# Row chunk by row chunk: another order for the matmuls of the last three hidden blocks

## The chip, the cores and the metric

The kernel runs on one core of a Trainium2 chip. The metric is the device time of one execution in microseconds (us): the median over several runs, set beside the kernel before it on the same chip. One further execution was recorded by the hardware profiler; every duration in this text comes from that recording.

## What is computed

The reference is one layer with two residual steps. The second is the one that matters here:

```python
x = x + tanh(g_xattn) * attention(layernorm(x), ctx, ...)
x = x + tanh(g_ffn) * ffn(layernorm(x), gate_w, w1, w2)

def ffn(x, gate_w, w1, w2):                 # x: (2, 2048, 512), 8 experts
    probs = softmax(einsum('ntd,ed->nte', x, gate_w))
    g, m = top_k(probs.transpose(0, 2, 1), 512)       # each expert picks 512 rows per batch item
    xin = x[batch, m]
    h = gelu(einsum('nekd,edf->nekf', xin, w1))       # 512 -> 2048
    h = einsum('nekf,efd->nekd', h, w2)               # 2048 -> 512
    return zeros.at[batch, m].add(g[..., None] * h)
```

The cross-attention and the choice of the rows take the first part of the kernel and are not touched.

## The kernel before, in words

**Tiling.** The experts' work is cut into 16 groups, one for each expert `e` and batch item `b` (`g = 2e + b`). A group has 512 rows, in `NC = 4` chunks of 128, and 2048 hidden columns, in `KF = 16` blocks of 128. Every float32 product is made as three matmuls from a high and a low part of each operand (high x high, high x low, low x high). From expert 1 on, the first GEMM (`products_pe`) makes the hidden values of both batch items at once; those of item 1 stay in the tile `hid1` until its second GEMM.

**The second GEMM** is `output_pe` (line 1308). One call takes one step `s`, which is one hidden block: it waits until the block's low part of the hidden values is there (`h_split`, line 1311) and, from step 4 on, until the block of `w2` has been split (`w2_low`, line 1317). Then it goes over the four chunks of rows. Each chunk has a PSUM bank of its own (`Y_BANKS[c]`), and three matmuls of 128 x 512 add into it. So a step is 12 matmuls, and each bank gets three of them in every step. What is told of them:

```python
                if s == KF - 1 and c < NC - 1:
                    last.then_inc(y_chunk, 1)
            last.then_inc(y_sum, 1)
```

The semaphore `y_chunk` tells that a chunk is finished, which happens only in step 15; `y_sum` counts finished steps, and its last value tells that chunk 3 is finished.

**Buffers.** The tiles `hh` (high part of the hidden values) and `w2hl` (both parts of `w2`) have four slots, taken in turn by `s % 4` and `f % 4`. Slot reuse is guarded by `y_sum`: `high_second_act` (line 1294) may write `hh` for step `s` once step `s - 4` is finished, and `w2_high_act` (line 1161) likewise. On ScalarE the high part of `w2` (line 1165) and then the high part of the hidden values (line 1298) are made; VectorE follows with the two low parts (lines 1170 and 1303). SyncE loads the blocks of `w2` ahead of them (line 1085). In item 1 the blocks are taken from 15 down to 0, so the last step, 15, works on block 0.

**The end of a group.** `output_rows` (line 1335) multiplies a chunk by its rows' gates, out of the bank into `y`: chunks 0 and 1 on ScalarE (line 1345), chunks 2 and 3 on VectorE (line 1347). Then `scatter_pool` (line 1423) on GpSimd adds the chunk to the output rows in device memory with one indirect DMA with addition (line 1430), whose descriptors GpSimd makes. The four scatters of a group stand in order in GpSimd's queue. Each first waits for its own chunk and for all scatters of the group before. After the last group's four scatters the kernel ends: SyncE waits for all of them to have landed (lines 1811 and 1812).

**Order.** Nothing plans the work at run time: each engine's order is the order of the calls in `expert_pe`, `expert_act`, `expert_dve`, `expert_pool` and `expert_sp`. In the call for expert 7 (`final`) no later expert's work is mixed in.

Of the kernel before, what the change touches and what calls it, by code (L numbers as in the profile page):

```python
# [16 lines left out]
P = 128  # L17
# [11 lines left out]
def wait(eng, sem, value):  # L29

    if not isinstance(value, int) or value > 0:
        eng.wait_ge(sem, value)
# [14 lines left out]
def flamingo_layer(nc, x, ctx_in, mask, g_xattn, g_ffn, Wq, bq, Wk, bk, Wv, bv, Wo, bo, gate_w, w1, w2, out):  # L47
# [5 lines left out]
    KF = F // P  # L53
# [5 lines left out]
    NC = CAP // P  # L59
# [19 lines left out]
    with whole:  # L79
        def sem(name):  # L80
            return whole.enter_context(nc.semaphore(name))

        def keep(name, shape, dt):
            return whole.enter_context(nc.sbuf_tensor(name, shape, dt))
# [69 lines left out]
        hid1_low = keep("hid1_low", [P, KF, CAP], F32R)  # L154
# [64 lines left out]
        w2hl = keep("w2hl", [P, 4, 2, D], F32R)  # L219
        HIGH, LOW = range(2)  # L220
# [4 lines left out]
        hh = keep("hh", [P, 4, CAP], F32R)  # L225
# [76 lines left out]
        h_split = sem("h_split")  # L302
# [7 lines left out]
        y_sum = sem("y_sum")  # L310
        y_chunk = sem("y_chunk")
# [642 lines left out]
        def choice_pe(pe, b, piece):  # L954
            if piece < STEPS:
                if b == 0 and piece == 0:
                    pe.wait_ge(consts, CONSTS)
                pe.wait_ge(bit_count, b * STEPS + piece + 1)
                total = CHOICE_BANK[:, 0:CANDS * E]
                if b == 0:  # L960
                    for t in range(TB):
                        last = pe.matmul(total.rearrange("p (c e) -> p c e", c=CANDS), ones_m[:, :],
                                         atleast[:, :, t, :],
                                         start=(t == 0), stop=(t == TB - 1))
                else:
                    last = pe.matmul(total, ones_m[:, :], count[:, :, :].rearrange("p c e -> p (c e)"),
                                     start=True, stop=True)
                last.then_inc(bit_total, 1)
            elif piece == STEPS:
                pe.wait_ge(pick_in, 3 * b + 1)  # L970
                running_place(pe, above, NE)
                pe.wait_ge(pick_in, 3 * b + 2)
                running_place(pe, tied, 0)
                pe.wait_ge(pick_in, 3 * b + 3)
                pe.matmul(CHOICE_BANK[:, 2 * NE:2 * NE + E], ones_m[:, :], count[:, 0, :], start=True, stop=True)\
                  .then_inc(pick_sum, 1)
# [22 lines left out]
        Y_BANKS = (bank[0], bank[1], bank[2], bank[3])  # L999
# [24 lines left out]
        TOKENS_AT = {1: 0, 4: 1, 7: 2, 10: 3}  # L1024
        PROMOTE_AT = 12
        RUN_ON = 2

        def is_plain(e):
            return isinstance(e, int) and e == 0
# [4 lines left out]
        def pairs_before(e, p):  # L1034
            return e * NP - NP + p

        def step_no(e, b, s):
            return e * 2 * KF + b * KF + s

        def block_of(e, b, s):  # L1040
            return s if is_plain(e) or b == 0 else KF - 1 - s
# [3 lines left out]
        def w2_no(e, b, f):  # L1045
            if is_plain(e):
                return KF * b + f
            return e * 28 + 4 + (f if b == 0 else KF + KF - 1 - REUSED - f)
# [24 lines left out]
        def wait_w2_low(eng, done):  # L1073

            if isinstance(done, int) and done <= W2_EARLY:
                wait(eng, w2_low_early, done)
            else:
                eng.wait_ge(w2_low, done - W2_EARLY)
# [215 lines left out]
        def high_second_act(act, e, s):  # L1294
            f = block_of(e, 1, s)
            act.wait_ge(c22_act if f % 2 else c12_act, pairs_before(e, f // 2) + 1)
            act.wait_ge(y_sum, step_no(e, 1, s) - 3)
            act.activation(hh[:, s % 4, :], hid1[:, f, :], ACT.Copy).then_inc(h_high, 1)  # L1298

        def split_second_dve(dve, e, s):  # L1300
            f = block_of(e, 1, s)
            dve.wait_ge(h_high, step_no(e, 1, s) + 1)
            dve.tensor_tensor(hid1_low[:, f, :], hid1[:, f, :], hh[:, s % 4, :].bitcast(F32), ALU.subtract)\  # L1303
               .then_inc(h_split, 1)
# [3 lines left out]
        def output_pe(pe, e, b, s, inside=None):  # L1308
            n, g = step_no(e, b, s), e * 2 + b
            f = block_of(e, b, s)  # L1310
            pe.wait_ge(h_split, n + 1)
            if is_plain(e) or b == 0:
                wait_w2_low(pe, w2_no(e, b, f) + 1)
                low = hid0_low[:, s % 4, :]
            else:
                if s >= REUSED:
                    wait_w2_low(pe, w2_no(e, b, f) + 1)
                low = hid1_low[:, f, :]
            for c in range(NC):
                if s == 0 and not (isinstance(g, int) and g == 0):  # L1320

                    pe.wait_ge(y_act if c < 2 else y_dve, g * 2 - 2 + c % 2 + 1)
                for hpart, part in ((HIGH, HIGH), (HIGH, LOW), (LOW, HIGH)):
                    high = hh[:, s % 4, c * P:(c + 1) * P]
                    last = pe.matmul(Y_BANKS[c][:, :], high if hpart == HIGH else low[:, c * P:(c + 1) * P],  # L1325
                                     w2hl[:, f % 4, part, :],
                                     start=(s == 0 and hpart == HIGH and part == HIGH),
                                     stop=(s == KF - 1 and hpart == LOW))
                if c == 0 and inside is not None:
                    choice_pe(pe, 1, inside)  # L1330
                if s == KF - 1 and c < NC - 1:
                    last.then_inc(y_chunk, 1)
            last.then_inc(y_sum, 1)

        def output_rows(eng, e, b, c, done):
            g = e * 2 + b
            if c < NC - 1:
                eng.wait_ge(y_chunk, g * (NC - 1) + c + 1)
            else:
                eng.wait_ge(y_sum, step_no(e, b, KF))  # L1340
            wait(eng, scattered[c], g * 16)
            eng.wait_ge(promoted[b], e + 1)
            gate = slot_gate[:, b, c:c + 1]
            if eng is nc.scalar:
                ins = eng.activation(y[:, c, :], Y_BANKS[c][:, :], ACT.Copy, scale=gate)  # L1345
            else:
                ins = eng.tensor_scalar(y[:, c, :], Y_BANKS[c][:, :], gate, None, ALU.mult)
            ins.then_inc(done, 1)
# [3 lines left out]
        def slots_pe(pe, g):  # L1352
            pe.wait_ge(hot, g + 1)
            for t in range(TB):
                last = pe.matmul(SLOT_BANK[:, 0:NC * NV], onehot[:, t, :],  # L1355
                                 carried[:, t, :, :].rearrange("p c v -> p (c v)"),
                                 start=(t == 0), stop=(t == TB - 1))
            last.then_inc(slots_sum, 1)
# [292 lines left out]
        def after_plain(e):  # L1651
            return isinstance(e, int) and e == 1
# [15 lines left out]
        def expert_pe(pe, e, final):  # L1668
            if not after_plain(e):
                products_pe(pe, e, 0)  # L1670
            for p in range(NP):
                if p + 1 < NP:
                    products_pe(pe, e, p + 1)
                if p in SLOTS_AT and not final:
                    pe.wait_ge(combined, (pairs_before(e, p) + 1) * COMBINED + U3_IS)
                    slots_pe(pe, e * 2 + 2 + SLOTS_AT[p])
                for s in (2 * p, 2 * p + 1):
                    output_pe(pe, e, 0, s)
            for s in range(KF):
                if s in TOKENS_AT and not final:  # L1680
                    operands_pe(pe, e + 1, TOKENS_AT[s])
                output_pe(pe, e, 1, s)

        def expert_act(act, e, final):
            if not after_plain(e):
# [4 lines left out]
            for p in range(NP):  # L1690
# [7 lines left out]
                if p + 1 < NP:  # L1698
                    for f in (2 * p + 2, 2 * p + 3):
                        w2_high_act(act, e, 0, f)  # L1700
                    hidden_act(act, e, p + 1)
            for s in range(RUN_ON):
                high_second_act(act, e, s)
            for c in (0, 1):
                output_rows(act, e, 0, c, y_act)
            for s in range(KF):
                if s in TOKENS_AT and not final:
                    operands_high_act(act, e + 1, TOKENS_AT[s])
                if s + RUN_ON < KF:
                    high_second_act(act, e, s + RUN_ON)  # L1710
                if 1 <= s <= KF - REUSED:
# [6 lines left out]
        def expert_dve(dve, e, final):  # L1718
# [4 lines left out]
            for p in range(NP):  # L1723
# [9 lines left out]
                if p in SLOTS_AT and not final:  # L1733
                    slots_dve(dve, e + 1, SLOTS_AT[p])
            for s in range(RUN_ON):
                split_second_dve(dve, e, s)
            for c in (2, 3):
                output_rows(dve, e, 0, c, y_dve)
            for s in range(KF):
                if s in TOKENS_AT and not final:  # L1740
                    operands_mix_dve(dve, e + 1, TOKENS_AT[s])
                if s + RUN_ON < KF:
                    split_second_dve(dve, e, s + RUN_ON)
                if 1 <= s <= KF - REUSED:
# [204 lines left out]
```

## Time and profile before

| | us |
|---|---|
| median of 3 runs | 1564.37 |
| lowest, highest | 1562.61, 1566.11 |
| the profiled execution: time | 1563.59 |
| the profiled execution: span | 1561.8 |
| TensorE busy in the span | 1493.4 |
| mean granted TensorE clock | 0.987 |

The span runs from the first to the last recorded event; 1.8 us of the profiled execution's time lie outside it. The profiled execution is 0.8 us below the median. A granted clock of 1.0 is TensorE's full 2.4 GHz, 0.5 is 1.2 GHz. Matmuls overlap at their ends, so the time between the starts of two of them is shorter than the duration that a row shows. The DMA share is the mean over the 16 DMA engines. It can read a little over 1 in a short window.

### The profile page before, as it was taken

What the parts mean: (1) busy time and instruction counts of PE and PEld (TensorE: products, weight loads), DVE (VectorE), ACT (ScalarE), POOL (GpSimd) and SP (SyncE); (2) the same over time, 40 slices, a digit from 0 to 9 for tenths busy, and PEclk for the clock granted to TensorE, in tenths of its full rate; (3) what the DMA queues carried; (4) which work ended last, traced back from release to release, by engine and by line L of the source; (5) the groups of instructions that cost most, each with busy time, mean ns of one, the idle gap of its engine ahead of it and who ended that gap; (6) DMA issues with size and microseconds to landing.
All of it is one profiled execution on the core that took longest, in us unless ns stands there. A gap on an engine that the chain in (4) does not pass through costs nothing.

```text
span 1561.8 us, 22316 instructions
## 1 busy us (share of the span) xinstructions
PE 1493.4 (96%) x7169; PEld 1211.2 (78%) x7169; DVE 1015.7 (65%) x1716; ACT 732.8 (47%) x1347; POOL 593.7 (38%) x554
## 2 busy tenths in 40 slices
PE   6886699999999999999999999999999999999996
PEld 5654477787788888888888888888888888888885
DVE  2578776657766676676657676767667675766542
ACT  1385233445444554454445444455445444554432
POOL 2265555543544044323443244403531444323211
PEclk9999699999999999999999999999999999999998
DMA  7176423543333333245234423334324433442133
GB/s 229 55 255 204 162 88 99 141 138 82 89 120 62 101 97 95 93 88 116 82 108 81 110 91 99 74 95 103 100 76 95 110 96 93 82 108 81 42 78 70
DMA packets 101401, 163.58 MB, mean 105 GB/s; under 512 B 7411, under 2 KB 45315, under 8 KB 101285
## 3 DMA queue, kind: packets, MB, share of 16 engines
q1 hardware_dynamic: 86885, 128.50, 26.4%
q0 software_dynamic: 14400, 33.56, 11.9%
q8 instruction: 69, 1.13, 0.3%
q14 instruction: 47, 0.39, 0.1%
HBM read 128.48 MB, written 33.55 MB: 104 GB/s over the span
## 4 chain that ended last, share of the span: by engine, by line
PE 86%; DVE 7%; issue 2%; ACT 2%; POOL 1%; DMA 1%; POOLq 0%; SPq 0%; DVEq 0%; ACTq 0%
PE bank L1325 42%; PE bank L1211 33%; PE bank L1185 4%; PE bank L1480 2%; PE bank L572 1%; PE bank L590 1%; PE bank L400 1%; DVE st L817 1%; DVE onehot L1366 1%; ACT xT L641 1%; DVE sc L793 0%; DMA ctx_raw<-in_ctx 0%; PE bank L1355 0%; DVE w2hl L1170 0%; DVE hid_low L1203 0%
## 5 line engine op out<-in xcount | busy, mean ns | idle before, releaser
L1325 PE MATMUL bank<-w2hl,hh 128*128 128x512 f32 x2048 | 635.7, 392 | 0.0
L1211 PE MATMUL bank<-xo,whl 128*128 128x512 f32 x2352 | 543.0, 390 | 3.7 <-DVE mix L1275 2.8
L1211 PEld LDWEIGHTS bank<-xo,whl 128*128 128x128 f32 x2352 | 440.7, 188 | 98.5 <-DVE mix L1275 3.7
L1325 PEld LDWEIGHTS bank<-w2hl,hh 128*128 128x128 f32 x2048 | 380.4, 188 | 76.0
L1325 PE MATMUL bank<-w2hl,hid_low 128*128 128x512 f32 x1024 | 398.7, 389 | 0.0
L1325 PEld LDWEIGHTS bank<-w2hl,hid_low 128*128 128x128 f32 x1024 | 192.2, 188 | 40.4
L1430 POOL DMA_INDIRECT layer_out<-y,slot_row x64 | 103.2, 1613 | 301.8 <-ACT y L1345 287.0
L1170 DVE TENSOR_TENSOR w2hl<-raw,w2hl 128x512 fp32r<-128x512 f32 x213 | 147.7, 715 | 50.6 <-ACT w2hl L1165 41.3
L1139 POOL TENSOR_TENSOR whl<-raw,whl 128x512 fp32r<-128x512 f32 x56 | 82.1, 1466 | 258.2 <-ACT whl L1105 258.2
L1165 ACT ACTIVATE w2hl<-raw 128x512 fp32r<-128x512 f32 x228 | 136.5, 624 | 60.1 <-DMA raw<-in_L_ffn_w 43.9
L1144 POOL TENSOR_TENSOR whl<-wsum,whl 128x512 fp32r<-128x512 f32 x56 | 75.1, 1341 | 183.4 <-ACT whl L1126 183.4
L1250 ACT ACTIVATE mix<-bank 128x512 f32<-128x512 f32 x56 | 33.4, 596 | 200.4 <-PE bank L1211 200.3
L1257 ACT ACTIVATE hid<-bank 128x512 f32<-128x512 f32 x56 | 33.5, 599 | 157.5 <-PE bank L1211 157.5
L1278 DVE TENSOR_TENSOR mix<-bank,mix 128x512 f32<-128x512 f32 x56 | 38.8, 692 | 96.4 <-PE bank L1211 96.2
L1185 PE MATMUL bank<-xp,whl 128*128 128x512 f32 x384 | 94.3, 396 | 1.6 <-DVE xp L1452 1.6
L1303 DVE TENSOR_TENSOR hid_low<-hid,hh 128x512 fp32r<-128x512 f32 x112 | 86.8, 779 | 12.8 <-ACT hh L1298 12.8
L1275 DVE TENSOR_TENSOR mix<-bank,mix 128x512 f32<-128x512 f32 x56 | 38.5, 688 | 80.4 <-PE bank L1211 80.4
L1185 PEld LDWEIGHTS bank<-xp,whl 128*128 128x128 f32 x384 | 73.2, 191 | 17.6 <-DVE xp L1452 2.3
L1283 DVE TENSOR_TENSOR hid<-bank,mix 128x512 f32<-128x512 f32 x56 | 38.7, 692 | 67.3 <-PE bank L1211 67.3
L1291 DVE TENSOR_TENSOR hid_low<-hid,hh 128x512 fp32r<-128x512 f32 x112 | 80.0, 714 | 1.0 <-ACT hh L1266 1.0
L1146 POOL TENSOR_TENSOR whl<-wsum,whl 128x512 fp32r<-128x512 f32 x56 | 76.4, 1364 | 0.0
L1126 ACT ACTIVATE whl<-wsum 128x1024 fp32r<-128x1024 f32 x56 | 59.0, 1054 | 36.7 <-DVE wsum L1122 36.7
(224 smaller groups left out, 1783.0 us busy)
## 6 DMA issues: line engine op xcount, KB each, us to landing
raw<-in_L_ffn_w SPq DMA_DIRECT2D x228, 256.0 KB, 2.7
raw<-in_L_ffn_w SPq DMA_DIRECT2D x72, 512.0 KB, 4.9
x_s<-in_x SPq DMA_DIRECT2D x8, 1024.0 KB, 6.9
layer_out<-x SPq DMA_DIRECT2D x8, 1024.0 KB, 9.0
xn_rows<-xn SPq DMA_DIRECT2D x8, 1024.0 KB, 4.9
raw_k<-in_L_xattn_Wk SPq DMA_DIRECT2D x1, 1024.0 KB, 5.4
raw_q<-in_L_xattn_Wq SPq DMA_DIRECT2D x1, 1024.0 KB, 11.3
raw_v<-in_L_xattn_Wv SPq DMA_DIRECT2D x1, 1024.0 KB, 13.4
```

Of the source, the lines that this page charges most:

```text
L1126: act.activation(whl[:, p % 2, HIGH, 2 * S1:14, :], wsum[:, :, :], ACT.Copy).then_inc(w1_sum_high, 1)
L1139: pool.tensor_tensor(low[:, 2 * A11:2 * A11 + 4, :], raw1[:, p % 2, :, 0:P], high[:, 2 * A11:2 * A11 + 4, :], ALU.subtract)
L1144: pool.tensor_tensor(low[:, 2 * S1:2 * S1 + 4, :], wsum[:, 0:4, :], high[:, 2 * S1:2 * S1 + 4, :], ALU.subtract)
L1146: pool.tensor_tensor(low[:, 2 * S3:2 * S3 + 4, :], wsum[:, 4:8, :], high[:, 2 * S3:2 * S3 + 4, :], ALU.subtract).then_inc(w1_low, 1)
L1165: act.activation(w2hl[:, f % 4, HIGH, :], raw2[:, slot, :], ACT.Copy).then_inc(w2_high, 1)
L1170: eng.tensor_tensor(w2hl[:, f % 4, LOW, :], raw2[:, slot, :], w2hl[:, f % 4, HIGH, :].bitcast(F32), ALU.subtract).then_inc(w2_low_early if ...
L1185: last = pe.matmul(H_BANKS[f % 2][:, :], whl[:, p % 2, part, 2 * k + f % 2, :], xp[:, b, xpart, k, :], start=(k == 0 and part == HIGH and ...
L1211: last = pe.matmul(bk[:, :], whl[:, p % 2, part, 2 * w + k, :], xo[:, xpart, x, k, :], start=(not adds and k == 0 and part == HIGH and xpa ...
L1291: dve.tensor_tensor(hid0_low[:, f % 4, :], hid0[:, f % 4, :], hh[:, f % 4, :].bitcast(F32), ALU.subtract)\
L1303: dve.tensor_tensor(hid1_low[:, f, :], hid1[:, f, :], hh[:, s % 4, :].bitcast(F32), ALU.subtract)\
L1325: last = pe.matmul(Y_BANKS[c][:, :], high if hpart == HIGH else low[:, c * P:(c + 1) * P], w2hl[:, f % 4, part, :], start=(s == 0 and hpar ...
L1430: pool.indirect_dma_start(out_rows, bass.IndirectOffsetOnAxis(ap=slot_row[:, b, c:c + 1], axis=0), y[:, c, :], None, compute_op=ALU.add).t ...
```

## The change

In the call for the last expert, item 1, steps 0 to 12 are as before. The 36 matmuls of steps 13, 14 and 15 are issued by a new function, `last_blocks_pe`, with the loops exchanged: chunk outside, step inside. It first waits for the hidden values and the `w2` blocks of all three steps, then adds nine matmuls into bank 0 and tells `y_chunk`, nine into bank 1, nine into bank 2, nine into bank 3. The last matmul of each step in chunk 3 raises `y_sum`. The number of matmuls, their operands and what each bank sums is the same, and within a bank so is the order. No other engine's program is changed.

```diff
+        ENDING = 3
...
+        def last_blocks_pe(pe, e):
+            ends = range(KF - ENDING, KF)
+            for s in ends:
+                pe.wait_ge(h_split, step_no(e, 1, s) + 1)
+                wait_w2_low(pe, w2_no(e, 1, block_of(e, 1, s)) + 1)
+            for c in range(NC):
+                cs = slice(c * P, (c + 1) * P)
+                for s in ends:
+                    f = block_of(e, 1, s)
+                    for hpart, part in ((HIGH, HIGH), (HIGH, LOW), (LOW, HIGH)):
+                        last = pe.matmul(Y_BANKS[c][:, :], hh[:, s % 4, cs] if hpart == HIGH else hid1_low[:, f, cs],
+                                         w2hl[:, f % 4, part, :], start=False, stop=(s == KF - 1 and hpart == LOW))
+                    if c == NC - 1:
+                        last.then_inc(y_sum, 1)
+                if c < NC - 1:
+                    last.then_inc(y_chunk, 1)
...
-            for s in range(KF):
+            for s in range(KF - ENDING if final else KF):
                 if s in TOKENS_AT and not final:
                     operands_pe(pe, e + 1, TOKENS_AT[s])
                 output_pe(pe, e, 1, s)
+            if final:
+                last_blocks_pe(pe, e)
```

TensorE before, from the start of step 13 of the last group (`bank0` to `bank3` are the banks of chunks 0 to 3, `hh` the high and `hid1_low` the low part of the hidden values):

```order
L1325 MATMUL bank0<-w2hl,hh 128x512 [waits w2_low,h_split]
L1325 MATMUL bank0<-w2hl,hh 128x512
L1325 MATMUL bank0<-w2hl,hid1_low 128x512
L1325 MATMUL bank1<-w2hl,hh 128x512 x2
L1325 MATMUL bank1<-w2hl,hid1_low 128x512
L1325 MATMUL bank2<-w2hl,hh 128x512 x2
L1325 MATMUL bank2<-w2hl,hid1_low 128x512
L1325 MATMUL bank3<-w2hl,hh 128x512 x2
L1325 MATMUL bank3<-w2hl,hid1_low 128x512
L1325 MATMUL bank0<-w2hl,hh 128x512 [waits w2_low,h_split]
```

The step gives three matmuls to each bank, and the next step begins with bank 0 and its own waits.

TensorE with the change, from the same place:

```order
L1348 MATMUL bank0<-w2hl,hh 128x512 [waits w2_low,h_split]
L1348 MATMUL bank0<-w2hl,hh 128x512
L1348 MATMUL bank0<-w2hl,hid1_low 128x512
L1348 MATMUL bank0<-w2hl,hh 128x512 x2
L1348 MATMUL bank0<-w2hl,hid1_low 128x512
L1348 MATMUL bank0<-w2hl,hh 128x512 x2
L1348 MATMUL bank0<-w2hl,hid1_low 128x512
L1348 MATMUL bank1<-w2hl,hh 128x512 x2
```

Bank 0 now gets nine matmuls before bank 1 gets its first, and the waits for all three steps stand ahead of the first.

TensorE with the change, at its very end:

```order
L1348 MATMUL bank2<-w2hl,hid1_low 128x512
L1348 MATMUL bank3<-w2hl,hh 128x512 x2
L1348 MATMUL bank3<-w2hl,hid1_low 128x512
L1348 MATMUL bank3<-w2hl,hh 128x512 x2
L1348 MATMUL bank3<-w2hl,hid1_low 128x512
L1348 MATMUL bank3<-w2hl,hh 128x512 x2
L1348 MATMUL bank3<-w2hl,hid1_low 128x512
```

Bank 3 gets all of its last nine matmuls at the end of the program, where before each bank had three of the last twelve.

## Rows read from the trace of the kernel before

**Rows 1.** The page: busy us and share of the span, then the chain's shares.
```profile
PE 1493.4 (96%) x7169; PEld 1211.2 (78%) x7169; DVE 1015.7 (65%) x1716; ACT 732.8 (47%) x1347; POOL 593.7 (38%) x554
...
PE 86%; DVE 7%; issue 2%; ACT 2%; POOL 1%; DMA 1%; POOLq 0%; SPq 0%; DVEq 0%; ACTq 0%
```

**Rows 2.** The chain that ended last, from 1540 us (start us, us, what).
```profile
1539.95 7.72 PE bank L1325 x34
...
1551.06 1.55 POOL layer_out L1430
...
1554.78 1.56 POOL layer_out L1430
```

**Rows 3.** Timeline, all engines, 1539 to 1562 us (start us, us, engine, line, operation).
```profile
1538.85 0.63 ACT L1165 ACTIVATE w2hl<-raw 128x512 fp32r<-128x512 f32 x1 [1.56 <-PE bank L1325]
...
1540.13 0.68 DVE L1303 TENSOR_TENSOR hid_low<-hid,hh 128x512 fp32r<-128x512 f32 x1
...
1541.15 0.41 PEld L1325 LDWEIGHTS bank<-w2hl,hh 128*128 128x128 f32 x2
1541.37 0.62 PE L1325 MATMUL bank<-w2hl,hh 128*128 128x512 f32 x2
...
1543.18 0.39 PE L1325 MATMUL bank<-w2hl,hid_low 128*128 128x512 f32 x1
...
1545.22 0.39 PE L1325 MATMUL bank<-w2hl,hid_low 128*128 128x512 f32 x1
...
1547.27 0.39 PE L1325 MATMUL bank<-w2hl,hid_low 128*128 128x512 f32 x1
...
1547.69 1.37 ACT L1345 ACTIVATE y<-bank,slot_gate 128x512 f32<-128x512 f32 x2 [7.69 <-PE bank L1325]
...
1549.05 1.43 DVE L1347 TENSOR_SCALAR y<-bank,slot_gate 128x512 f32<-128x512 f32 x2 [8.24 <-PE bank L1325]
...
1549.20 1.55 POOL L1430 DMA_INDIRECT layer_out<-y,slot_row  x1 [35.62 <-ACT y L1345]
1549.31 0.39 PE L1325 MATMUL bank<-w2hl,hid_low 128*128 128x512 f32 x1
```

**Rows 4.** Lines 1345 and 1347 in the last 22 us (ns min/median/max, first and last start).
```profile
L1345 ACT ACTIVATE y<-bank,slot_gate x2: 689/689/689, 1547.7 to 1548.4; 128x512 f32<-128x512 f32 x2
L1347 DVE TENSOR_SCALAR y<-bank,slot_gate x2: 751/751/751, 1549.1 to 1549.7; 128x512 f32<-128x512 f32 x2
```

**Rows 5.** Windows 1549.2 to 1559.9 us: length, five engines' busy us, PEclk, DMA share, GB/s.
```profile
1549.20:1551.30 2.10, 0.49 (x3) 0.07 (x1) 1.28 (x2) 0.00 (x0) 1.79 (x2) 1.00 0.00 0
1551.30:1559.90 8.60, 0.00 (x0) 0.00 (x0) 0.00 (x0) 0.00 (x0) 4.43 (x3) 0.56 0.98 123
```

**Rows 6.** Line 1430, the last group's first two scatters: issue to landing.
```profile
DMA to landing us min/median/max: 5.2/5.4/5.5
```

**Rows 7.** Line 1430, its last two scatters: issue to landing.
```profile
DMA to landing us min/median/max: 5.7/5.7/5.7
```

**Rows 8.** Chain of GpSimd, 313 to 316 us: twelve matmuls into one bank.
```profile
313.01 2.72 PE bank L1185 x12
```

**Rows 9.** Line 1085, the last load of a w2 block (ns, start; us to landing).
```profile
L1085 SPq DMA_DIRECT2D raw<-in_L_ffn_w x1: 328/328/328, 1534.8 to 1534.8; - x1
...
DMA to landing us min/median/max: 2.6/2.6/2.6
```

**Rows 10.** Line 1085, all 228 loads of a w2 block: us to landing.
```profile
DMA to landing us min/median/max: 2.5/2.7/6.9
```

**Rows 11.** Windows after the last matmul, columns as in rows 5.
```profile
1551.00:1552.00 1.00, 0.00 (x0) 0.00 (x0) 0.00 (x0) 0.00 (x0) 0.94 (x1) 1.00 0.98 72
...
1552.50:1553.00 0.50, 0.00 (x0) 0.00 (x0) 0.00 (x0) 0.00 (x0) 0.19 (x2) 0.50 1.08 197
```

**Rows 12.** Timeline of TensorE, 183 to 187 us, at a granted clock of 0.50.
```profile
183.17 4.13 PE L1185 MATMUL bank<-xp,whl 128*128 128x512 f32 x9 [1.56 <-DVE xp L1452]
```

## The prediction

> **What bounds the kernel now.** The page comes first. TensorE is busy for 96% of the span and is 86% of the chain that ended last [rows 1], so anywhere in the middle only TensorE's own time counts, and the change leaves its 36 matmuls what they were. The end of the chain tells something else [rows 2]: TensorE's last piece in it ends at 1547.67 us, and after that only GpSimd appears, with scatters at 1551.06 and 1554.78 us. TensorE itself works on until 1549.31 + 0.39 = 1549.70 us [rows 3]. So the last chunk's matmuls are not what the end waits for: the end waits for four scatters in a row, and these wait for chunk 0.
>
> The timeline of the last 23 us shows why [rows 3]. All four chunks are finished within the last step: chunk 0 at 1547.27 + 0.39 = 1547.66 us, chunk 3 at 1549.70 us, 2.04 us apart. Eviction on ScalarE starts 0.03 us after chunk 0's last matmul, takes 0.69 us [rows 3, 4], and the first scatter starts at 1549.20 us, 0.82 us after it. The scatters follow each other by (1554.78 - 1549.20) / 3 = 1.86 us [rows 2, 3]. GpSimd has every later chunk ready before it can take it; it is a queue that began too late.
>
> Below the scatters lie the DMA engines. They move nothing until 1551.30 us, 2.10 us after the first scatter's start, and are then 98% busy for 8.60 us [rows 5]. Four scatters in 8.60 us are 2.15 us each, more than the 1.86 us between two issues, so work piles up in front of them. The first two scatters land 5.5 and 5.2 us after their starts, the last two 5.7 us [rows 6, 7]. The last lands at 1554.78 + 5.7 = 1560.48 us, and 1.3 us later the span of 1561.8 us ends.
>
> **The change, step by step.** Matmuls start (1549.31 - 1541.37) / 35 = 0.227 us apart [rows 3]. Exchanging the loops leaves the 36 starting points and gives them to other chunks: chunk 0 has the first nine, and so on. Every ninth one is a row of the timeline, which gives the new finishing times: chunk 0 at 1543.18 + 0.39 = 1543.57, chunk 1 at 1545.22 + 0.39 = 1545.61, chunk 2 at 1547.66, chunk 3 at 1549.70 us as before. Chunk 0 gains 4.09 us, chunk 3 nothing.
>
> *The new waits.* Steps 14 and 15 must be ready before step 13 starts. The last thing that they need is the low part of step 15's hidden values, finished at 1540.13 + 0.68 = 1540.81 us; the first weight load of step 13 is at 1541.15 us [rows 3]. That is 0.34 us to spare, so I cost the waits at nothing, with 0 to 0.3 us as bounds (six semaphore waits in a row, at the 0.03 us that a hand-over took above, are 0.2). Behind these waits stand only TensorE's last 36 matmuls. ScalarE and VectorE have nothing between 1540.81 us and the evictions, so nobody is held up by the later end of steps 13 and 14.
>
> *Nine matmuls into one bank.* Twelve in a row into one bank took 2.72 us [rows 8], which is 12 x 0.227: the same pace as over four banks. Cost nothing; bounds 0 and, at a rounding of 0.01 in 2.72 us, 0.03 us. The Trainium skill says otherwise (Perfetto Trace Analysis, Matmul Optimizations): all eight PSUM banks should be in use to have as much parallelism as possible. By that rule grouping nine on one bank would slow TensorE, by a price the page doesn't give. This trace does not agree at these sizes.
>
> *The scatters.* Each starts at the later of two times: its own chunk's finish + 0.03 + eviction (0.69 on ScalarE, 0.75 on VectorE [rows 4]) + 0.82, or 1.86 us after the scatter before it.
> Scatter 0: 1543.57 + 1.54 = 1545.11.
> Scatter 1: 1545.61 + 1.54 = 1547.15 (queue 1546.97).
> Scatter 2: 1547.66 + 1.60 = 1549.26 (queue 1549.01).
> Scatter 3: 1549.70 + 1.60 = 1551.30 (queue 1551.12).
> The last scatter starts 1554.78 - 1551.30 = 3.48 us earlier. From there TensorE is the bound again: chunk 3's last matmul, its eviction, its scatter.
>
> *The landing of the last scatter.* Here the trace leaves a choice. If it again takes 5.7 us, the gain is 3.48 us. If the DMA engines set the end, their 8.60 us begin at 1545.11 + 2.10 = 1547.21 and end at 1555.81 instead of 1559.90 us: 4.09 us. Scatters now come 2.06 us apart, nearly the engines' own 2.15, so the last one meets a backlog of 1547.21 + 3 x 2.15 - (1551.30 + 2.10) = 0.26 us, where it had 1551.30 + 3 x 2.15 - (1554.78 + 2.10) = 0.87 us. I take the middle, 3.8 us, because the first scatter, with no backlog at all, still took 5.5 us, only 0.2 less than the last.
>
> Sum: 0 (waits) + 0 (bank) - 3.8 us. The span becomes 1558.0 us, the profiled execution 1563.59 - 3.8 = 1559.8 us, and from the median, 0.8 us above that execution, 1564.37 - 3.8 = **1560.6 us**. What a measurement of this kernel can tell from no change is about 0.2%, 3.1 us; the three runs of before lie 3.5 us apart. The gain stands just above it.
>
> **The rivals.**
> *A: no backlog counts, 3.5 us.* For it: two scatters with little in front of them took 5.5 and 5.2 us and the two behind them 5.7, so what a scatter takes hardly depends on the backlog. Against: 98% busy engines for 8.60 us. Time: 1564.37 - 3.48 = 1560.9 us. The Trainium skill (DMA: Bandwidth & Descriptors, Anatomy of one DMA) has it this way: a fixed 2.0 us and the bytes at 436 GB/s, an estimate of 2.6 us for a scatter of 262,144 bytes, with 0.6 us of moving, so engines idle between issues. This trace shows 123 GB/s and 5.2 us at least.
>
> *B: the gathered wait is late, or hand-overs are slower than 0.82 us.* With 0.34 us to spare every delay of step 15's operands now goes straight to the end. The last `w2` load starts at 1534.8 and lands in 2.6 us, at 1537.4; ScalarE takes it at 1538.85 us [rows 3, 9]. Loads took up to 6.9 us [rows 10]. One that long would land at 1541.7, shift the operands by 2.85 us and hold TensorE for 2.5 us: gain 1.3 us, 1563.1 us. Against: the long ones lie beside scatters, and none is under way there. Two slow hand-overs of 0.8 us each would leave 2.2 us, 1562.2 us.
>
> *C: nothing is gained.* If GpSimd's start were held by something other than chunk 0 (the four waits for the scatters before, the gates' order), the four scatters would stay where they are: 1564.4 us. For it: the 0.82 us between eviction and scatter are unexplained. Against: they follow the eviction at once, after 35.62 us of waiting for ScalarE [rows 3].
>
> *D: slower, by the clock.* After its last matmul at 1549.70 us TensorE's granted clock was still 1.00 up to 1552.0 and 0.50 (1.2 GHz) from 1552.5 us [rows 11], so an idle time of 2.3 to 2.8 us halves it. At 0.50 nine matmuls took 4.13 us [rows 12], 0.459 each, 0.232 more than now. If B's hold of 2.5 us reaches that point, the 36 matmuls cost up to 36 x 0.232 = 8.4 us more: -3.8 + 2.5 + 8.4 = +7.1, 1571.5 us. It decides from a hold of 2.3 us on, if more than 19 of the 36 then run at half clock (2.5 + 19 x 0.232 - 3.8 = 3.1). Before the change the same late load would have had 5.4 us more room.
>
> **How the numbers follow.** Forecast 0.45, A 0.25, B 0.15, C 0.08, D 0.03; the 0.04 left is for a gain beyond 4.5 us. The forecast and A differ by 0.3 us and stand 0.4 to 0.7 us above the bound of 3.1; with medians that wander by about 1 us, some 0.85 of their 0.70 is measured as faster, 0.60, and with the 0.04 that is 0.64. B, C and the rest of the forecast and A are within 0.2%: 0.33. D is 0.03. The range takes the forecast with the ends 3.48 and 4.09, 1 us of measurement on both sides and most of B: 1559.0 to 1563.0 us. Left out are C, D and a bit of each tail.
>
> **What would show it.** In the profile after: the span ends 8.3 us after TensorE's last matmul, not 12.1; scatters start 2.0 to 2.1 us apart instead of 1.86, each 0.8 us behind an eviction; the chain's end runs through chunk 3's matmuls, VectorE's eviction and one scatter. The last landing takes 5.1 to 5.7 us, which tells the forecast from A. A gap on TensorE ahead of step 13 shows B; a granted clock below 1.00 before the last matmul shows D; scatters still 1.86 us apart and ending at the same time show C. I am wrong if the last scatter doesn't start 3.2 us or more earlier against TensorE's last matmul.

## The result, and the profile after

| | before | with the change |
|---|---|---|
| median, us | 1563.05 (10 runs) | 1559.09 (10 runs) |
| profiled execution: time, us | 1563.59 | 1557.74 |
| profiled execution: span, us | 1561.8 | 1555.9 |
| its last matmul ends, us | 1549.70 | 1547.77 |
| from there to the span's end (the tail), us | 12.10 | 8.13 |

The ratio is 0.9973, with a 95% interval of 0.9963 to 0.9983: 4.2 us less, between 2.7 and 5.8 us. The seven further runs of the kernel before brought its median from 1564.37 to 1563.05 us. One of them took 1906.81 us; it is not in the ratio, and the other nine runs, 1561.80 to 1566.11 us, have a median of 1562.74 us. Spans are read to 0.1 us, so a tail is good to about 0.05 us.

The page still names TensorE. Two lines of it, to be laid beside [rows 1] (busy us and share of the span; shares of the chain):

```profile
PE 1491.1 (96%) x7169; PEld 1209.0 (78%) x7169; DVE 1015.3 (65%) x1716; ACT 733.1 (47%) x1347; POOL 593.3 (38%) x554
...
PE 86%; DVE 7%; ACT 2%; issue 2%; POOL 1%; DMA 1%; POOLq 0%; SPq 0%; DVEq 0%; ACTq 0%
```

The middle hardly moved (0.6 us, worked out below). The timeline of the end, all engines (start us, us, engine, line, operation), answers to [rows 3]. The functions behind the new code have moved by 20 lines: 1345, 1347 and 1430 of before are 1365, 1367 and 1450 here.

```profile
1539.22 0.39 PE L1326 MATMUL bank<-w2hl,hid_low 128*128 128x512 f32 x1
...
1539.45 0.62 PE L1348 MATMUL bank<-w2hl,hh 128*128 128x512 f32 x2
...
1541.26 0.39 PE L1348 MATMUL bank<-w2hl,hid_low 128*128 128x512 f32 x1
...
1541.69 0.69 ACT L1365 ACTIVATE y<-bank,slot_gate 128x512 f32<-128x512 f32 x1 [3.61 <-PE bank L1348]
...
1543.20 1.55 POOL L1450 DMA_INDIRECT layer_out<-y,slot_row  x1 [31.54 <-ACT y L1365]
1543.30 0.39 PE L1348 MATMUL bank<-w2hl,hid_low 128*128 128x512 f32 x1
...
1545.24 1.55 POOL L1450 DMA_INDIRECT layer_out<-y,slot_row  x1 [0.49 <-issue]
1545.34 0.39 PE L1348 MATMUL bank<-w2hl,hid_low 128*128 128x512 f32 x1
...
1545.77 0.75 DVE L1367 TENSOR_SCALAR y<-bank,slot_gate 128x512 f32<-128x512 f32 x1 [6.88 <-PE bank L1348]
...
1547.34 1.56 POOL L1450 DMA_INDIRECT layer_out<-y,slot_row  x1 [0.55 <-DMA layer_out<-y,slot_row]
1547.38 0.39 PE L1348 MATMUL bank<-w2hl,hid_low 128*128 128x512 f32 x1
1547.81 0.75 DVE L1367 TENSOR_SCALAR y<-bank,slot_gate 128x512 f32<-128x512 f32 x1 [1.29 <-PE bank L1348]
1549.38 1.56 POOL L1450 DMA_INDIRECT layer_out<-y,slot_row  x1 [0.48 <-issue]
```

Step 13's first matmul starts at 1539.45 us, 0.23 us after step 12's last: no gap. The ninth matmul of each chunk ends at 1541.26 + 0.39 = 1541.65, then 1543.69, 1545.73 and 1547.77 us, 2.04 us apart. Each eviction starts 0.04 us after its chunk, and the first scatter 0.82 us after its eviction. Scatters follow each other by 2.04, 2.10 and 2.04 us. The last one starts 1.61 us after the last matmul; before it was 5.08 us after it. So it moved by 3.47 us, where 3.48 was worked out.

The windows of the DMA engines' work (length; busy us of TensorE, its weight loads, VectorE, ScalarE and GpSimd; granted clock; DMA share; GB/s) answer to [rows 5]:

```profile
1543.20:1545.30 2.10, 2.10 (x11) 1.75 (x10) 0.00 (x0) 0.69 (x1) 1.61 (x2) 1.00 0.00 0
1545.30:1553.90 8.60, 2.47 (x11) 1.69 (x10) 1.50 (x2) 0.00 (x0) 4.61 (x3) 0.76 0.96 122
```

The engines again begin 2.10 us after the first scatter's start and are busy for 8.60 us, 96% instead of 98%. Against the last matmul this stretch ends at 6.13 us instead of 10.20: 4.07 us earlier.

The chain that ended last needs a caution here (start us, us, what), beside [rows 2]:

```profile
1539.61 2.06 PE bank L1348 x9
...
1541.69 0.70 ACT y L1365
...
1543.20 4.15 DMA layer_out<-y,slot_row
1547.35 1.29 POOL layer_out L1450
```

It goes from chunk 0's nine matmuls over the first scatter's DMA to a later scatter. The program has no wait of one scatter for another of the same group; the scatter at 1547.34 us stands 0.82 us behind its own eviction, 1545.77 + 0.75. A landing merely fell into the same moment. The releasers in a chain are inferred, and this one is wrong. So the prediction's sign that the chain would end over chunk 3's matmuls, VectorE's eviction and one scatter did not appear; the timeline above shows that order, with 0.04 and 0.82 us between the three.

The span of this execution is 5.9 us shorter, but only 12.10 - 8.13 = 3.97 us of it is the tail. The other 1.9 us do not come from the end: the part before the experts was 2.5 us shorter, where no line of the change runs, and the middle gave 0.6 us back. The first row of the tile `onehot` in each of four executions, whose "first start" (167.7, 165.2, ...) marks the beginning of the experts' part: the kernel before, the change, the change with two steps (below), and the change once more:

```profile
L1366 DVE TENSOR_TENSOR onehot<-iota_slot,slot_lo x16: 2282/2284/3379, 167.7 to 1273.8; 128x2048 bf16<-128x2048 bf16 x16
L1386 DVE TENSOR_TENSOR onehot<-iota_slot,slot_lo x16: 2282/2285/3376, 165.2 to 1271.9; 128x2048 bf16<-128x2048 bf16 x16
L1386 DVE TENSOR_TENSOR onehot<-iota_slot,slot_lo x16: 2282/2284/3376, 168.7 to 1275.4; 128x2048 bf16<-128x2048 bf16 x16
L1386 DVE TENSOR_TENSOR onehot<-iota_slot,slot_lo x16: 2282/2284/3378, 164.9 to 1271.9; 128x2048 bf16<-128x2048 bf16 x16
```

The last matmul of these four ends at 1549.70, 1547.77, 1551.27 and 1547.79 us. Less the first start, that is 1382.0, 1382.6, 1382.6 and 1382.9 us. One execution differs from another by up to 4 us in its first 170 us, and by at most 0.9 us from there to the last matmul. So from here on the tail is compared, which leaves this out, beside the times.

### The profile page after: what moved, and what is told of

Its sections match the earlier page's. It is cut to its first block, busy times and chain, and to the rows that moved or that the text cites. A ratio compares the mean times of both kernels' runs of the same rounds, so it can differ in the third digit from the quotient of the medians.

```text
span 1555.9 us, 22316 instructions
## 1 busy us (share of the span) xinstructions
PE 1491.1 (96%) x7169; PEld 1209.0 (78%) x7169; DVE 1015.3 (65%) x1716; ACT 733.1 (47%) x1347; POOL 593.3 (38%) x554
## 4 chain that ended last, share of the span: by engine, by line
PE 86%; DVE 7%; ACT 2%; issue 2%; POOL 1%; DMA 1%; POOLq 0%; SPq 0%; DVEq 0%; ACTq 0%
PE bank L1326 42%; PE bank L1212 33%; PE bank L1186 4%; PE bank L1500 2%; PE bank L572 1%; PE bank L590 1%; DVE onehot L1386 1%; DVE st L817 1%; PE bank L400 1%; ACT xT L641 1%; DVE hid_low L1204 0%; DVE sc L793 0%; PE bank L1375 0%; DMA ctx_raw<-in_ctx 0%; DVE w2hl L1171 0%
## 5 line engine op out<-in xcount | busy, mean ns | idle before, releaser
L1326 PE MATMUL bank<-w2hl,hh 128*128 128x512 f32 x2024 | 628.4, 392 | 0.0
L1326 PEld LDWEIGHTS bank<-w2hl,hh 128*128 128x128 f32 x2024 | 376.0, 188 | 75.1
L1326 PE MATMUL bank<-w2hl,hid_low 128*128 128x512 f32 x1012 | 394.0, 389 | 0.0
```

## The experiments

All tails in one place. "Start" is the last scatter's start after the last matmul's end, "spacing" the time from the scatter before it, "issue to end" the tail less the start.

| run | spacing | start | tail | issue to end |
|---|---|---|---|---|
| before | 1.87 | 5.08 | 12.10 | 7.02 |
| waits only | 1.87 | 5.09 | 12.05 | 6.96 |
| two steps | 1.86 | 3.04 | 9.93 | 6.89 |
| the change | 2.04 | 1.61 | 8.13 | 6.52 |
| the change again | 2.04 | 1.61 | 8.31 | 6.70 |
| chunk wait last, first scatter | 2.05 | 1.62 | 8.33 | 6.71 |
| chunk wait last, later three | 2.04 | 1.70 | 8.32 | 6.62 |
| chunk wait last, all four | 2.04 | 1.70 | 8.15 | 6.45 |
| staggered | 2.72 | 1.61 | 7.83 | 6.22 |
| four steps | 2.72 | 1.62 | 7.78 | 6.16 |
| the change, last scatter alone | none | 1.61 | 7.64 | 6.03 |
| before, last scatter alone | none | 1.61 | 7.60 | 5.99 |

**Two steps.**

```diff
-        ENDING = 3
+        ENDING = 2
```

> Only steps 14 and 15 are exchanged (24 matmuls), not 13. With tail = time from the last matmul's end to the end of the span (12.1 us before, 8.1 us with the change). Chunk 0 is then finished 12 matmuls earlier than before, 2.72 us, chunk 1 8 matmuls... in full: first scatter 2.05 us earlier (chunk 0 after 6 of 24 matmuls: 9 x 0.227), and as chunks now come 1.36 us apart, the queue of scatters at 1.86 us is the limit again. Theory (the end follows the first scatter, through the DMA engines' 8.6 us): tail 12.1 - 2.05 = 10.05 us. Rival A (the end follows the last scatter's start, fixed landing): last scatter also 2.05 us earlier, the same 10.05. Rival C (order alone does nothing, the 4 us come from elsewhere): tail 12.1 or 8.1. Time 2 us below the kernel before.

(Its "12 matmuls earlier" for chunk 0 is a slip; nine matmuls, 2.05 us, is the difference, and the tail is worked out from that.)

Measured: tail 9.93 us, median 1560.68 us (8 runs), ratio 0.9982 (0.9971 to 0.9993), 2.8 us less than before. The timeline of GpSimd shows the queue (start us, us, ...; the third scatter is left out):

```profile
1548.73 1.55 POOL L1450 DMA_INDIRECT layer_out<-y,slot_row  x1 [33.58 <-ACT y L1365]
1550.59 1.55 POOL L1450 DMA_INDIRECT layer_out<-y,slot_row  x1 [0.30 <-issue]
...
1554.31 1.56 POOL L1450 DMA_INDIRECT layer_out<-y,slot_row  x1 [0.30 <-issue]
```

Scatters are 1.86 us apart: chunks finish faster than GpSimd issues, and it is a queue with an earlier start again. So 12.10 - 9.93 = 2.2 of the 4 us come from exchanging two steps, the rest from the third. Rival C is gone: the tail follows the number of steps exchanged.

**Four steps.**

```diff
-        ENDING = 3
+        ENDING = 4
```

> Four steps are exchanged, 12 to 15. The wait ahead of step 12 then needs step 15's hidden values, which are ready 2.0 us after step 11's end. Rival D and B's mechanism: TensorE idles 2.2 to 2.4 us ahead of step 12 (0 with the change as it is). If the granted clock stays at 1.00, the 48 matmuls keep 0.227 us and the end comes 2.2 to 2.4 us later than with three steps, less 0.1 to 0.3 us for a backlog that is gone: about 2.0 us below the kernel before. If the idle time halves the clock, the 48 matmuls cost up to 48 x 0.232 = 11 us more and the kernel is slower than before. I expect the clock to stay: tail 7.8 to 8.1 us.

Measured: tail 7.78 us, median 1562.11 us (10 runs), ratio 0.9994 (0.9984 to 1.0003). The timeline of TensorE at step 11's end and step 12's start:

```profile
1539.93 0.39 PE L1326 MATMUL bank<-w2hl,hid_low 128*128 128x512 f32 x1
1542.56 0.70 PE L1348 MATMUL bank<-w2hl,hh 128*128 128x512 f32 x2 [2.24 <-DVE hid_low L1304]
```

The idle time is 2.24 us, and what ended it is the hidden values' low part, as expected. The two windows that hold it and the 48 matmuls behind it (columns as above):

```profile
1540.00:1542.60 2.60, 0.36 (x3) 0.07 (x1) 1.29 (x2) 1.15 (x2) 0.00 (x0) 1.00 0.01 3
1542.60:1553.70 11.10, 11.10 (x48) 8.86 (x48) 0.75 (x1) 1.38 (x2) 4.18 (x3) 1.00 0.37 45
```

The granted clock stays at 1.00 in both. The 48 matmuls take 11.1 us, 0.23 each, so the hold costs its own length and not a doubled matmul time. In the times four steps give back most of the gain: 0.9 us below the kernel before by the ratio (between 2.5 less and 0.5 more), an interval that holds the 2.0 us expected; by the profile it is 12.10 - 7.78 - 2.24 = 2.1 us. Three is the largest number of steps that this order can take without a hold.

The same execution shows a scatter with nothing in front of it, though three went before. The DMA engines had run dry by the time the last scatter's data moved, 2.1 us after its start at 1555.34 us (columns as above):

```profile
1557.12:1557.22 0.10, 0.00 (x0) 0.00 (x0) 0.00 (x0) 0.00 (x0) 0.00 (x0) 1.00 0.00 0
...
1557.42:1557.52 0.10, 0.00 (x0) 0.00 (x0) 0.00 (x0) 0.00 (x0) 0.00 (x0) 1.00 3.50 143
```

**Waits only.** The steps in the old order behind the gathered waits:

```diff
-            for c in range(NC):
-                cs = slice(c * P, (c + 1) * P)
-                for s in ends:
-                    f = block_of(e, 1, s)
+            for s in ends:
+                f = block_of(e, 1, s)
+                for c in range(NC):
+                    cs = slice(c * P, (c + 1) * P)
...
-                    if c == NC - 1:
-                        last.then_inc(y_sum, 1)
-                if c < NC - 1:
-                    last.then_inc(y_chunk, 1)
+                    if s == KF - 1 and c < NC - 1:
+                        last.then_inc(y_chunk, 1)
+                last.then_inc(y_sum, 1)
```

> The waits of steps 13 to 15 all stand ahead of step 13, but the steps are taken as before. If the gathered waits cost nothing (0.34 us to spare), step 13's first matmul starts 0.227 us after step 12's last, and the tail is that of before, 12.1 us. If they cost, there is a gap ahead of step 13 of up to 0.3 us. The tail can't be 8.1 us if the order of the matmuls is what gains.

Measured: tail 12.05 us. TensorE's timeline, step 12's last matmul and step 13's first:

```profile
1539.70 0.39 PE L1326 MATMUL bank<-w2hl,hid_low 128*128 128x512 f32 x1
1539.93 0.62 PE L1348 MATMUL bank<-w2hl,hh 128*128 128x512 f32 x2
```

They start 0.23 us apart. The waits cost nothing, and without the exchanged loops they gain nothing.

**One scatter alone**, with the change and with the kernel before. The edit is the same in both:

```diff
-                for c in range(NC):
-                    scatter_pool(pool, e, 1, c)
+                scatter_pool(pool, e, 1, NC - 1)
...
-                sp.wait_ge(scattered[c], 16 * G)
+                sp.wait_ge(scattered[c], 16 * G if c == NC - 1 else 16 * G - 16)
```

> With the change, but the last group's scatters of chunks 0, 1 and 2 are left out (their rows lack the last expert's part). Nothing lies in front of the last scatter in the DMA engines. Theory (a backlog of about 0.26 us in front of the last scatter): tail 8.1 - 0.3 = 7.8 us, and the engines busy for about 2.15 us from 2.1 us after its start. Rival A (a scatter takes what it takes): tail 8.1 us. If the engines need less than 2.15 us for one scatter alone, then the rate of 122 GB/s was not theirs but that of the issues.

> The kernel before, with the last group's scatters of chunks 0, 1 and 2 left out (their rows lack the last expert's part). Chunk 3's last matmul is the last of all, as with the change, so if the order of the matmuls acts only through the scatters in front, the tail is the same as with the change and one scatter: 7.6 us, against 12.1 us with four scatters. If the old order costs anything else at the end, the tail is longer than 7.8 us.

Measured: tails of 7.64 and 7.60 us. The scatter with the change, and the windows after its start:

```profile
1549.77 1.55 POOL L1450 DMA_INDIRECT layer_out<-y,slot_row  x1 [37.73 <-DVE y L1367]
```

```profile
1549.80:1551.80 2.00, 0.00 (x0) 0.00 (x0) 0.00 (x0) 0.00 (x0) 1.52 (x1) 0.80 0.02 4
1551.80:1554.10 2.30, 0.00 (x0) 0.00 (x0) 0.00 (x0) 0.00 (x0) 0.00 (x0) 0.50 0.93 114
```

A single scatter begins in the DMA engines 2.0 us after its start and keeps them 93% busy for 2.30 us at 114 GB/s. So the rate of 122 GB/s in the full rows is the engines' own, not that of the issues, and a scatter every 1.86 us is more than they take. The tail of 7.64 us is 0.2 us under the 7.8 us of the theory and 0.5 us under rival A's 8.1 us. That the old and the new order agree, where with four scatters they lie 4 us apart, says that the order of the matmuls acts on the tail through the scatters in front, to within the 0.2 us to which a tail repeats (below).

**GpSimd's waits in another order.** Three kernels, for all four scatters of the last group, for the later three, and for the first:

```diff
+            chunk_last = isinstance(e, int) and e + 1 == E and b == 1
+            if not chunk_last:
+                pool.wait_ge(y_act if c < 2 else y_dve, g * 2 + c % 2 + 1)
-            pool.wait_ge(y_act if c < 2 else y_dve, g * 2 + c % 2 + 1)
             for other in range(NC):
                 wait(pool, scattered[other], g * 16)
             pool.wait_ge(promoted[b], e + 1)
+            if chunk_last:
+                pool.wait_ge(y_act if c < 2 else y_dve, g * 2 + c % 2 + 1)
```

(and with `and c > 0`, or `and c == 0`, behind the first line.)

> With the change, and in the last group's four scatters GpSimd's wait for the chunk stands behind the waits for the earlier scatters and the gates, not ahead of them. If most of the 0.82 us from eviction to scatter is GpSimd working through those waits, the hand-over falls to 0.3 to 0.4 us, every scatter starts 0.4 to 0.5 us earlier against the last matmul, and by both theories (first scatter and DMA engines, or last scatter) the tail falls from 8.1 to 7.6 or 7.7 us. If the 0.82 us are something else, nothing moves. The time can't tell this from the change (0.03%), the tail can; against the kernel before it should be about 4.4 us faster.

> The same exchange of waits for the scatters of chunks 1, 2 and 3 only. The first scatter stays, the last starts 0.45 us earlier (1.15 us after the last matmul instead of 1.6). Rival A (the end follows the last scatter's start with a fixed landing): tail 8.1 - 0.45 = 7.7 us. Theory (DMA engines busy for 8.6 us from 2.1 us after the first scatter): the engines' stretch stays, tail 8.0 to 8.1 us.

> The exchange of waits for the first scatter only. The first scatter starts 0.45 us earlier, the last stays at 1.6 us after the last matmul. Rival A: tail 8.1 us. Theory: the engines' stretch begins 0.45 us earlier and ends so, until the last scatter alone is the bound (7.64 us, measured with it alone): tail 7.7 us.

> The change as it is, once more, for how much the tail itself moves from one execution to another: 8.1 us, within 0.1 to 0.2 us. If it moves more than 0.3 us, the two experiments with single waits can't tell the theories apart.

The idea behind them failed. With the wait for the chunk last, for all four (timeline: eviction and scatter of chunks 0 and 3):

```profile
1541.87 0.69 ACT L1365 ACTIVATE y<-bank,slot_gate 128x512 f32<-128x512 f32 x1 [3.60 <-PE bank L1348]
...
1543.47 1.55 POOL L1454 DMA_INDIRECT layer_out<-y,slot_row  x1 [31.63 <-ACT y L1365]
...
1547.99 0.75 DVE L1367 TENSOR_SCALAR y<-bank,slot_gate 128x512 f32<-128x512 f32 x1 [1.29 <-PE bank L1348]
1549.65 1.56 POOL L1454 DMA_INDIRECT layer_out<-y,slot_row  x1 [0.48 <-issue]
```

From the first eviction's end, 1541.87 + 0.69 = 1542.56 us, to the scatter at 1543.47 us it is 0.91 us, and for chunk 3 from 1548.74 to 1549.65 the same 0.91: 0.09 us more than with the change, not 0.4 less. GpSimd had its other waits behind it and still needed 0.91 us from the eviction's end to the scatter, so working through them is not what the time is made of. So the scatters were not moved, and the two kernels that were to tell the forecast from rival A tell nothing. The change once more has a tail of 8.31 us, so a tail moves by 0.2 us from one execution to another, and all four kernels of this group lie within that. The time of the first, a median of 1557.95 us (5 runs) and a ratio of 0.9965 (0.9952 to 0.9979), is not distinct from the change's.

**Staggered.** What the failed pair was to show needs another spacing of the scatters. Four steps, in an order that lets chunk 0 finish much earlier without waiting for step 15's operands at the start:

```diff
-        ENDING = 3
+        ENDING = 4
...
+            for s in range(a, z):
+                ready(s)
+                three(0, s)
+            three(1, a)
+            ready(z)
+            three(0, z).then_inc(y_chunk, 1)
+            for c in range(1, NC):
+                for s in range(a + (c == 1), KF):
+                    last = three(c, s)
                     if c == NC - 1:
                         last.then_inc(y_sum, 1)
                 if c < NC - 1:
                     last.then_inc(y_chunk, 1)
```

(`a` is 12, `z` is 15, `ready` holds the two waits of a step, `three` the three matmuls of a chunk and step.)

> Steps 12 to 15 (48 matmuls) with chunks that finish further apart and no hold on TensorE: chunk 0's steps 12, 13, 14, then chunk 1's step 12, and only then chunk 0's step 15, which is the first that needs the operands that come last. Chunks 0 to 3 finish 33, 24, 12 and 0 matmuls before the last, 7.5, 5.4, 2.7 and 0 us. Theory (the last scatter is delayed only by what lies in front of it in the DMA engines): with the scatter before it 2.72 us earlier, not 2.04, its issue-to-end falls from 6.5 to 6.7 us to about 6.16 us as in the run with four steps, tail 7.8 us and no gap of 2.2 us on TensorE. That is 0.4 us less than the change (8.1 to 8.3 us), too little for the times to tell; against the kernel before 4.4 us, ratio 0.997. Rival A: tail 8.1 to 8.3 us as with the change.

Measured: tail 7.83 us, median 1558.76 us (6 runs), ratio 0.997 (0.9958 to 0.9982). TensorE has no gap at the start of the four steps, and the four scatters on GpSimd come 2.04, 2.79 and 2.72 us apart:

```profile
1538.30 0.39 PE L1326 MATMUL bank<-w2hl,hid_low 128*128 128x512 f32 x1
1538.52 0.61 PE L1346 MATMUL bank<-w2hl,hh 128*128 128x512 f32 x2
```

```profile
1543.63 1.55 POOL L1459 DMA_INDIRECT layer_out<-y,slot_row  x1 [30.18 <-ACT y L1374]
...
1545.67 1.55 POOL L1459 DMA_INDIRECT layer_out<-y,slot_row  x1 [0.49 <-issue]
...
1548.46 1.56 POOL L1459 DMA_INDIRECT layer_out<-y,slot_row  x1 [1.23 <-DMA layer_out<-y,slot_row]
...
1551.18 1.56 POOL L1459 DMA_INDIRECT layer_out<-y,slot_row  x1 [1.16 <-DVE y L1376]
```

The last scatter starts 1.61 us after the last matmul, exactly as with the change, and yet the end comes 0.3 to 0.5 us sooner. What differs is what lies in front of it. This is one execution, and 0.3 us is not far above the 0.2 us to which a tail repeats; it counts together with the four steps, whose last scatter has the same spacing and nearly the same issue to end. It is the shortest tail of all the kernels that compute everything without holding TensorE. In the times it can't be told from the change (0.9970 and 0.9973), so it is a version at least as good, not one shown to be faster.

## Why the prediction was right, and where it was not

**What bounds the kernel.** Right. The end waited for four scatters that began with chunk 0. The last scatter alone gives 7.60 us with the old order, where four gave 12.10.

**The new finishing times and the last scatter's start.** Right: 3.48 us worked out, 3.47 seen, with 1.61 us from last matmul to last scatter.

**The waits, and nine matmuls into one bank.** Both cost nothing, as taken. The steps are 2.04 us apart for nine matmuls, the old 0.227 us each; the waits alone leave the tail at 12.05 us. The prediction weighed a rule of the Trainium skill (Perfetto Trace Analysis, Matmul Optimizations), to use all eight banks, and drew from it that nine in a row on one bank might slow TensorE. The measurement decides against that at this shape of matmul: 36 in a row into four banks by nines run at the pace of the old order.

**The landing of the last scatter.** The forecast took 0.3 us for the smaller backlog, rival A none. The table settles it against A: issue to end is 6.0 us with no scatter in front, 6.16 to 6.22 with 2.72 us of spacing, 6.45 to 6.71 with 2.04, 6.89 to 7.02 with 1.86. Twelve executions stand in the order that a backlog gives, and none falls out of it. Neighbouring groups lie about as close as a tail repeats, 0.2 us; the whole way from 6.0 to 7.0 us does not. From 1.86 to 2.04 us the mean falls from 6.96 to 6.60 us, 0.36 us. The tail as a whole gained 3.97 us in the first execution and 3.79 in the second, around the forecast of 3.8.

The size is another matter. The prediction's own backlogs, 0.87 and 0.26 us, differ by 0.61 us and not by 0.36; 3.8 us was the middle of two values between which it could not choose, and that the middle came out is partly luck. Beside the 6.0 us of a scatter alone, 0.26 us of backlog should give 6.27 us where 6.60 was measured, and with the DMA engines run dry in front of it, as with four steps, it should be 6.0 where it was 6.16. What the other 0.2 to 0.3 us are is open.

The sign that was to tell the forecast from A, a last landing of 5.1 to 5.7 us, could not be read: the profile after has no landing for the last scatter. Where a profile has it, the span ends 1.3 us after it (12.10 - 5.08 - 5.7 before, 7.83 - 1.61 - 4.9 staggered, 7.60 - 1.61 - 4.7 with one scatter in the old order). The landings of these last two:

```profile
DMA to landing us min/median/max: 4.9/4.9/4.9
...
DMA to landing us min/median/max: 4.7/4.7/4.7
```

With 1.3 us taken off its issue to end, the change's last scatter lands after an estimated 5.2 and 5.4 us in its two executions, against 5.7 us before. A scatter alone lands after 4.7 us, so the 5.5 us of the first scatter before, which the prediction held against the backlog, was not the time of an undisturbed one.

By the same rows the Trainium skill's sum for one DMA (DMA: Bandwidth & Descriptors, Anatomy of one DMA), from which the prediction had the DMA engines idle between issues, does not hold for this scatter with addition. They were 93% busy for 2.30 us with one of them, where the estimate had 0.6 us of moving, and it landed after 4.7 us, where the estimate had 2.6 us.

**B and D.** No hold came, since 0.34 us to spare were enough. The run with four steps made one of 2.24 us. Its price was its length, about 2 us, and the clock stayed. That is just short of the 2.3 us from which D was to decide. But D's 2.3 to 2.8 us came from one execution. In the twelve profiled executions the granted clock fell 2.0 to 5.4 us after the last matmul (last section), so that bound was too firm: the change's own execution lost the full clock after a shorter idle time than the 2.24 us that four steps withstood. The ten executions with four steps took 1561.26 to 1564.09 us, so none of them paid the up to 11 us that its expectation gave for a halved clock. Longer holds stay untried.

**C.** Excluded by two steps, three steps and the single scatter.

**What was off** is the level. "From the median, 1564.37 - 3.8" put the forecast on a median of three runs, and "1 us of measurement on both sides" was all that the range allowed for it. The median of ten runs of the same kernel is 1563.05 us, 1.3 us lower. From there the forecast would have been 1559.3 us, and 1559.09 was measured. As it stands, the measured median is 1.5 us below the forecast and lies 0.1 us inside the range's low end of 1559.0; the ratio times 1563.05 gives 1558.8 us, outside it. The term that failed is that 1 us, together with the 1564.37 us that it stood around. The 1558.8 us are 1564.37 less 1.3 for the base and 4.2 for the gain, where the range's low end allowed 1.0 for the base and 4.09 for the gain. The gain was sized well (3.8 forecast; 4.2, between 2.7 and 5.8, by the ratio; 3.8 to 4.0 by the tails), but the base moved by more than the range had room for, and the table of the three runs, 3.5 us apart, already said that it could. Three later series of the kernel before had medians of 1563.46 (17 runs), 1562.99 (9) and 1563.47 us (10), so it was the median of three that stood high. This says nothing against the mechanism: the failed step is how well the starting time was known.

The 0.82 us from eviction to scatter, which the prediction called unexplained and took as fixed, are still unexplained: the runs only exclude that they are GpSimd's working through the waits that stand behind the one for the chunk.

## What to carry to other kernels

When the last step of an accumulation finishes all its output tiles together and a slow serial stage follows (here scatters, 2.15 us each in the DMA engines), exchange the loops of the last few steps so that the tiles finish as far apart as the serial stage takes one. How many steps can be exchanged is set by the time at which the last step's operands are ready: one step too many held TensorE for 2.24 us and gave most of the gain back, and a staggered order took the same four steps without a hold. The four slots of `hh` set another limit, by the program: a fifth step could not be ready before the first is finished. For a change at the end of a kernel, compare the time from the last matmul to the end, which here repeated to 0.2 us, while whole executions differ by several us.

## What the runs showed of the hardware

A hold of 2.24 us on TensorE in the midst of dense matmuls left the granted clock at 1.00. After the last matmul of the execution with the change, at 1547.77 us, it was 1.00 until 1549.7 and 0.50 from 1549.9 us, 2.1 us later:

```profile
1547.80:1549.70 1.90, 0.00 (x0) 0.00 (x0) 0.75 (x1) 0.00 (x0) 1.42 (x2) 1.00 0.94 126
...
1549.90:1550.10 0.20, 0.00 (x0) 0.00 (x0) 0.00 (x0) 0.00 (x0) 0.20 (x1) 0.50 0.66 51
```

The same kernel once more kept 1.00 for 4.9 us after its last matmul, which ended at 1547.79 us:

```profile
1552.59:1552.69 0.10, 0.00 (x0) 0.00 (x0) 0.00 (x0) 0.00 (x0) 0.00 (x0) 1.00 0.99 102
...
1552.79:1552.89 0.10, 0.00 (x0) 0.00 (x0) 0.00 (x0) 0.00 (x0) 0.00 (x0) 0.50 0.77 123
```

In the kernel before it was 1.00 until 1552.0 us and 0.50 from 1552.5 [rows 11], 2.3 to 2.8 us later. Over the twelve profiled executions the fall came between 2.0 us (two steps, the change) and 5.4 us (chunk wait last, all four) after the last matmul. So idle times of about the same length came out either way, 2.24 us is no safe length, and a bound from one trace is good for that trace.

One indirect scatter with addition of 128 rows of 2 KB keeps the 16 DMA engines 93% busy for 2.30 us alone, and four of them take 8.60 us together, 2.15 us each. From the end of an eviction to the start of the scatter it takes GpSimd 0.8 to 0.9 us, whichever wait stands last.
